# Four edits in a one-core graph network: spare rows for pad slots, a later turn in the mixer, clears inside the rests of GpSimd, and another opening order of the second attend pass

## The reference, cut to what matters

```python
xn = layernorm(x)
x  = x + gnn0(xn, src, dst, edge_weight) + mix0(xn)   # mix0: 4 layers of linear attention and feed-forward
x  = x + moe(layernorm(x))                            # 8 experts, top 2
xn = layernorm(x)
x  = x + gat1(xn, edges (src -> dst)) + mix1(xn)      # gat1: softmax over the edges of each row; mix1: one layer
x  = x + ffn1(layernorm(x))                           # half of the tokens only
```

## Time and profile before

| | us |
|---|---|
| median of 3 runs | 5937.94 (5934.52 to 5938.88) |
| the profiled execution: own time | 5937.63 |
| its span, first to last instruction | 5935.8 |
| busy: TensorE | 5210.6 (88%) |
| busy: GpSimd | 3923.0 (66%) |
| busy: DVE | 3351.1 (56%) |
| busy: ScalarE | 2918.8 (49%) |

### The profile page before, as it was taken

One profiled execution on the slowest core, in us unless ns is written; L12 is line 12 of the kernel. 1 busy time (PEld: TensorE's weight loads), 2 busy tenths in 40 slices (PEclk: granted clock), 3 DMA queues, 4 the chain that ended last, 5 costly groups with the idle time before them and its releaser, 6 DMA issues. The chain is left out here.

```text
span 5935.8 us, 89987 instructions
## 1 busy us (share of the span) xinstructions
PE 5210.6 (88%) x25856; PEld 4404.4 (74%) x25856; DVE 3351.1 (56%) x8788; ACT 2918.8 (49%) x7114; POOL 3923.0 (66%) x6674
## 2 busy tenths in 40 slices
PE   5579999999989999899867999996877887777899
PEld 2468887888878888788756888884556666666788
DVE  8667775444545555443325555555767777776641
ACT  6345554555545555555434333332545555555444
POOL 1677787777666666777747777777457777777000
PEclk8799999999999999999978999997889999999999
DMA  2322112113333333344355122213323343336300
GB/s 68 91 77 52 50 45 64 42 50 111 104 113 95 103 97 103 105 113 113 103 66 158 49 59 54 59 49 97 79 77 104 103 107 103 104 103 96 98 24 33
DMA packets 378209, 493.21 MB, mean 83 GB/s; under 512 B 97664, under 2 KB 315640, under 8 KB 375288
## 3 DMA queue, kind: packets, MB, share of 16 engines
q0 software_dynamic: 135008, 236.92, 16.8%
q1 hardware_dynamic: 242712, 250.54, 14.4%
HBM read 385.16 MB, written 102.04 MB: 82 GB/s over the span
## 5 line engine op out<-in xcount | busy, mean ns | idle before, releaser
L305 POOL DMA_INDIRECT edges_g<-xn_rows,edges_idx x880 | 863.0, 981 | 390.5 <-issue 230.8
L2060 POOL DMA_INDIRECT messages_g<-h_rows,edges_record x880 | 842.9, 958 | 360.1 <-issue 231.0
L248 POOL DMA_INDIRECT sorted_dst<-edges_record,edges_place x784 | 800.8, 1021 | 365.8 <-issue 217.1
L248 POOL DMA_INDIRECT sorted_src<-edges_record,edges_place x784 | 770.6, 983 | 293.9 <-issue 213.7
L1224 PE MATMUL mixer_f_ps<-mixer_f_out,mixer_w 128*128 128x250 f32 x3200 | 755.6, 379 | 16.9 <-issue 15.7
L1235 PE MATMUL mixer_y_ps<-mixer_w,mixer_g 128*125 128x256 f32 x3200 | 724.6, 379 | 0.0
L277 POOL MEMSET edges_idle<- 128x96 f32 x3328 | 621.0, 187 | 144.3
L1224 PEld LDWEIGHTS mixer_f_ps<-mixer_f_out,mixer_w 128*128 128x128 f32 x3200 | 604.6, 193 | 87.1 <-issue 19.0
L1235 PEld LDWEIGHTS mixer_y_ps<-mixer_w,mixer_g 128*125 128x125 f32 x3200 | 593.8, 188 | 85.5
L2232 PE MATMUL messages_s_ps<-messages_g,messages_one 128*128 128x257 f32 x1760 | 456.3, 403 | 112.0 <-DVE messages_one L2143 105.6
L1381 ACT ACTIVATE mixer_g<-mixer_f_ps,mixer_b 128x250 f32<-128x250 f32 x800 | 330.3, 465 | 394.5 <-PE mixer_f_ps L1224 392.6
(11 more groups left out here) (543 smaller groups left out, 10403.2 us busy)
## 6 DMA issues: line engine op xcount, KB each, us to landing
mixer_q<-qT SPq DMA_DIRECT2D x100, 250.0 KB
mix_rows<-mixer_rows SPq DMA_DIRECT2D x100, 250.0 KB
qT<-mixer_qT SPq DMA_DIRECT2D x75, 250.0 KB, 2.9
mixer_rows<-mix_rows SPq DMA_DIRECT2D x75, 250.0 KB
edges_g<-xn_rows,edges_idx POOLq DMA_INDIRECT x880, 3.1
messages_g<-h_rows,edges_record POOLq DMA_INDIRECT x880
sorted_dst<-edges_record,edges_place POOLq DMA_INDIRECT x784
sorted_src<-edges_record,edges_place POOLq DMA_INDIRECT x784
```

The source lines that it names most:

```text
L248: self.nc.gpsimd.indirect_dma_start(self.orders[s][0], bass.IndirectOffsetOnAxis(self.place[s][:, j:j + 1], 0), self.record[s][:, j, :], N ...
L305: self.nc.gpsimd.indirect_dma_start(self.g[n % GR][:, j, 0:D], None, self.table_d, bass.IndirectOffsetOnAxis(self.idx[:, t:t + 1], 0)).the ...
L2060: self.nc.gpsimd.indirect_dma_start(self.g[n % GR][:, j, :], None, self.table_d, bass.IndirectOffsetOnAxis(self.idx[:, t:t + 1], 0)).then_inc(
```

## The change

It makes four edits. (1) Pad slots point at 128 rows of zeros behind row N, one for each lane, in both tables. (2) In the mixer, TensorE does `raise_part(1)` ahead of `rows_turned`, and ScalarE `curve(1)` ahead of `attend_affine`. (3) The two memsets of the sums are gone; the memsets of the rests clear the sums piece by piece (96 columns each) and go on with `idle` once they are through. (4) In `attend_low` SP loads what the fold needs first, the fold comes first on TensorE and DVE, the lists' PSUM tiles are others, and the last steps of the lists (now `look_listed`) stand on DVE at the end of chunk 0.

```diff
-    def pool_pause(self, pool):
-        for _ in range(PAUSES):
+    def pool_pause(self, pool, row=None):
+        sums, width = self.acc[:, :, :].rearrange("p h d -> p (h d)"), HB * (D + 1)
+        for k in range(PAUSES):
             if self.pauses:
                 pool.wait_ge(self.idled, self.pauses)
-            self.nc.gpsimd.memset(self.idle[:, :], 0.0).then_inc(self.idled, 1)
+            at = width if row is None else (row * PAUSES + k) * IDLE
+            tile = self.idle[:, :] if at >= width else sums[:, at:min(at + IDLE, width)]
+            self.nc.gpsimd.memset(tile, 0.0).then_inc(self.idled, 1)
...
         pool.dma_start(rec[:, :, :], self.orders[1][0].rearrange("(p t) c -> p t c", p=P)).then_inc(self.listed, 16)
-        nc.gpsimd.memset(self.acc[:, :, :], 0.0).then_inc(self.listing, 1)
...
+            sp.dma_start(spare[:, :], c_d["iota"][0:1, :].rearrange("o p -> p o")).then_inc(spare_in, 16)
             for to, src in ((kin[1], keys[1]), (win, weights)):
...
-            sp.wait_ge(blanked, 2)
+            sp.wait_ge(blanked, 4)
             for s in S:
                 sp.dma_start(orders[s][0].rearrange("(p t) c -> p t c", p=P), blank[:, :, :]).then_inc(edges.prefilled, 16)
+            sp.dma_start(table_d[N:N + P, :], zeros[:, 0:D]).then_inc(edges.prefilled, 16)
+            sp.dma_start(table2_d[N:N + P, :], zeros[:, :]).then_inc(edges.prefilled, 16)
...
-                    nc.vector.memset(blank[:, :, 1:3], 0.0).then_inc(blanked, 1)
+                    nc.vector.memset(blank[:, :, 2:3], 0.0).then_inc(blanked, 1)
                     nc.vector.memset(blank[:, :, 0:1], -1.0).then_inc(blanked, 1)
+                    nc.vector.memset(zeros[:, :], 0.0).then_inc(blanked, 1)
+                    dve.wait_ge(spare_in, 16)
+                    nc.vector.tensor_scalar(blank[:, :, 1], spare[:, 0:1].to_broadcast([P, ST]), float(N), None, ALU.add).then_inc(blanked, 1)
...
-            nc.gpsimd.memset(edges.acc[:, :, :], 0.0).then_inc(cleared, 1)
-            pool.wait_ge(cleared, 1)
...
+                    if forward:
+                        raise_part(p, m, 1)
                     if attend:
                         rows_turned(n)
-                    if forward:
-                        raise_part(p, m, 1)
                     side(0)
...
                         curve(p, m, 0)
+                    if forward:
+                        curve(p, m, 1)
                     if attend:
                         attend_affine(p, n)
-                    if forward:
-                        curve(p, m, 1)
```

In `attend_low` (SP, then DVE; `first_loads` are ident, wx, 16 pieces of the query and key weights, bx, gain and offset; `loads` are wo, blocks, bo and 8 pieces of wv):

```diff
-            for b in range(3):
+            sp.dma_start(x[0][:, :, :], rows_of(x_d, 0)).then_inc(x_loaded[0], 16)
+            sp.wait_ge(by_head, 2)
+            for to, src in first_loads:
+                sp.dma_start(to[:], src).then_inc(fold_in, 16)
+            for b in range(1, 3):
                 sp.dma_start(x[b][:, :, :], rows_of(x_d, b)).then_inc(x_loaded[b], 16)
...
             for b in range(2):
                 dve.wait_ge(x_loaded[b], 16)
                 ln.dve_stats(dve, b, b)
...
-            dve.wait_ge(listed, 6 * 16)
+            dve.wait_ge(fold_in, 16 * len(first_loads))
+            dve.wait_ge(started, 5)
+            for k in range(2):
+                nc.vector.tensor_scalar(wide_b[:, k, :], ones[:, :], bx[:, k:k + 1], None, ALU.mult).then_inc(prepared, 1)
+            for b in range(2):
+                ln.dve_norm(dve, b, b)
+            dve.wait_ge(listed, 5 * 16)
...
                 if c + 2 < NCH:
                     ln.dve_norm(dve, c + 2, b)
+                if c == 0:
+                    look_listed()
```

More of the change, by code:

```diff
@@ L352, in pairs_of, with open_stage @@
     return pairs[k * share:(k + 1) * share]
-def open_stage(nc, name, x_d, table_d, keys, weights, orders, edges, c_d):
+def open_stage(nc, name, x_d, table_d, table2_d, keys, weights, orders, edges, c_d):
     S = range(2)
@@ L373, in open_stage @@
             "ident_in", "key_in", "turned", "statted", "aggred", "rooted", "inverted", "normed"))
-        blank = ph.sb("blank", [P, ST, 3])
+        blank, spare, zeros, spare_in = ph.sb("blank", [P, ST, 3]), ph.sb("spare", [P, 1]), ph.sb("zeros", [P, D + 2]), ph.sem("spare_in")
         tally_at, before, spot, ahead = ph.sb("tally_at", [P, 2 * FAR + HB], BF16), ph.sb("before", [P, P], BF16), ph.sb("spot", [ROWS2, HB], BF16), ph.sb("ahead", [HB, ROWS2])
@@ L421, in _ @@
                 sp.dma_start(orders[s][1].rearrange("(p j) -> p j", j=PB), bucket_i[s][0:NB, :]).then_inc(saved, 16)
[L422 removed]
+            sp.wait_ge(edges.prefilled, 64)
             sp.wait_ge(saved, 32)
@@ L1711, in queries_turned @@
                 mm.then_inc(qT_made, 1)
-            pe.wait_ge(listed, 6 * 16)
-            pe.wait_ge(lists, 1)
-            nc.tensor.transpose(low_ps[0:1, 0:NT], low[:, :], ident[0:NT, 0:NT]).then_inc(found0, 1)
-            pe.wait_ge(lists, 6)
-            nc.tensor.matmul(low_ps[:, 64:65], spare[0:1, :], least[0:1, 0:1], start=True, stop=True).then_inc(found0, 1)
-            nc.tensor.matmul(a1_ps[:, 0:NPR], a1_rows[:, :], is_bucket[:, :], start=True, stop=True).then_inc(found0, 1)
-            pe.wait_ge(weights, 16 * len(loads))
+            pe.wait_ge(fold_in, 16 * len(first_loads))
             for i in range(2):
@@ L1730, in _ @@
             mm.then_inc(prep, 1)
-            pe.wait_ge(viewed, 1)
             ln.pe_turn(pe, 0, 0)
+            pe.wait_ge(listed, 5 * 16)
+            pe.wait_ge(lists, 1)
+            nc.tensor.transpose(low_ps[0:1, 0:NT], low[:, :], ident[0:NT, 0:NT]).then_inc(found0, 1)
+            pe.wait_ge(lists, 6)
+            nc.tensor.matmul(low_ps[:, 64:65], spare[0:1, :], least[0:1, 0:1], start=True, stop=True).then_inc(found0, 1)
+            nc.tensor.matmul(a1_ps[:, 0:NPR], a1_rows[:, :], is_bucket[:, :], start=True, stop=True).then_inc(found0, 1)
             pe.wait_ge(folded, 2)
@@ L1772, in _ @@
             pe.wait_ge(fed_plus, 1)
+            pe.wait_ge(weights, 16 * len(loads))
             for k in range(2):
@@ L1800, in _ @@
             act.wait_ge(ln.eps_ready, 1)
-            act.wait_ge(weights, 16 * len(loads))
+            ln.act_root(act, 0, 0)
+            act.wait_ge(fold_in, 16 * len(first_loads))
             act.wait_ge(prep, 1)
@@ L1912, in _ @@
-            step(nc.vector.tensor_tensor(rest[:, :], a1_t, look[:, :, 0], ALU.subtract))
-            dve.wait_ge(lists, 11)
-            step(nc.vector.tensor_copy(look[:, :, 1], rest[:, :]))
-            dve.wait_ge(lists, 12)
-            step(nc.vector.tensor_tensor(look[:, :, 2], rest[:, :], look[:, :, 1], ALU.subtract))
-            dve.wait_ge(lists, 13)
-            dve.wait_ge(weights, 16 * len(loads))
-            dve.wait_ge(started, 5)
-            for k in range(2):
-                nc.vector.tensor_scalar(wide_b[:, k, :], ones[:, :], bx[:, k:k + 1], None, ALU.mult).then_inc(prepared, 1)
@@ L1922, in _, with look_listed @@
-            for k in range(2):
-                nc.vector.tensor_scalar(diag[:, k, :], ident[:, :], bo[:, k:k + 1], None, ALU.mult).then_inc(started, 1)
-            for b in range(2):
-                ln.dve_norm(dve, b, b)
+            def look_listed():
+                dve.wait_ge(found0, 3)
+                dve.wait_ge(lists, 8)
+                dve.wait_ge(edge0, 6)
+                nc.vector.tensor_copy(a1_t, a1_ps[:, 0:NPR]).then_inc(viewed, 1)
+                dve.wait_ge(viewed, 1)
+                step(nc.vector.tensor_scalar(ms.a1_c[:, :], a1_t, shift[:, 1:2], None, ALU.add))
+                step(nc.vector.tensor_copy(look[:, :, 0], a1_t))
+                dve.wait_ge(lists, 10)
+                step(nc.vector.tensor_tensor(rest[:, :], a1_t, look[:, :, 0], ALU.subtract))
+                dve.wait_ge(lists, 11)
+                step(nc.vector.tensor_copy(look[:, :, 1], rest[:, :]))
+                dve.wait_ge(lists, 12)
+                step(nc.vector.tensor_tensor(look[:, :, 2], rest[:, :], look[:, :, 1], ALU.subtract))
+                dve.wait_ge(lists, 13)
+                dve.wait_ge(weights, 16 * len(loads))
+                for k in range(2):
+                    nc.vector.tensor_scalar(diag[:, k, :], ident[:, :], bo[:, k:k + 1], None, ALU.mult).then_inc(started, 1)
```

52 lines of the change are left out of this document (23 added, 29 removed).

## The result

The changed kernel takes 5847.61 us (median of 4 runs, 5843.5 to 5850.48), the kernel before 5936.23 in the same runs: ratio 0.9851, 95% interval 0.9837 to 0.9864, so 88.6 us less. The forecast was 5846. In later runs, beside experiments, the two kernels took 5847.41 and 5942.16 (ratio 0.984, 0.9827 to 0.9854).

What follows compares the result with a forecast made beforehand. TensorE was taken to bound the mixer and slow DMA landings its end. The terms -43 - 10.5 - 27 - 6.5 - 8 + 3 = -92, from a median of 5937.94, gave 5846 us; range 5825 to 5878.

Steps and rivals of the forecast that it cites:

- Part 1: Mixer's end: pads on 128 rows land in 2.8 us, not 14.0, removing TensorE's stall; -43, ends -30 and -46.
- The forecast's 1.3: Mixer's end: the margin in us by which GpSimd's own rate just doesn't bind once the gathers land fast.
- Rival (a): Mixer's and forward's ends: pads are slow at any address, so 38.5 us of gain goes, giving 5899; chance 0.08.
- Part 2: Forward stage's end: faster pad gathers and no GpSimd waits on TensorE bring the last batch earlier; -10.5 (-6 to -12).
- Part 3: Mixer's passes: raise_part ahead of rows_turned cuts TensorE's 37.7 us of waits for normed rows; -27, ends -29 and -12.
- the forecast's sign: Mixer: if right, the waits of L793 on the norm are under 10 us in all.
- the 1.7 set aside for `queries_kept`: Mixer: 1.5 to 2 us expected lost because ScalarE makes `queries_kept` later; taken off the 37.7 us of waits.
- rival (b): Another limiter: `queries_kept` late (+15), GpSimd's rate at mixer's end (+13), or fold's opening (+3); 5859 to 5877; chance 0.22.
- the forecast's own 72 turns: Mixer: count of turns with an attention part where TensorE might wait for ScalarE's attend_affine, in the slower-than-before rival, chance 0.03.
- Part 4: Removed memsets: DVE's open-stage chain shortens, -6.5; at the experts' end the next stage begins earlier, -8 (-6 to -10).
- Part 5: Second attend pass's opening: chunk 0 begins 1.6 earlier, but the lists' last steps stand uncovered on DVE; +3 (-3 to +6).

Runs made afterwards that it cites:

- e11: The changed kernel itself with all four edits, run again beside later experiments: 5847.41 us, against 5942.16 for the kernel before (ratio 0.984).
- e6: All four edits, but every pad slot points at the first spare row alone: 6546.58 us, on a chip slower for the kernel before.
- e8: All four edits, but the pad slot of lane p points at live row p, not a spare row: 6501.55 us, same slow chip.
- e9: All four edits, but the pads share 16 spare rows, eight lanes to a row: one run of 5855.05 us.
- e12: All four edits, but x(1) is loaded right behind x(0) and the lists' last DVE steps are spread: 5844.7 us.
- e10: All four edits, but ScalarE keeps its old order, attend_affine then curve(1): 5874.52 us, against 5847.41 for all four edits.
- e1: The kernel before with edit (1) alone, pads at spare rows in both tables: ratio 0.995 against 6586.49 us.
- e2: The kernel before with edit (2) alone, the order in the mixer on TensorE and ScalarE: ratio 0.9959 against 6586.49 us.
- e3: The kernel before with edit (3) alone, clears within the rests: ratio 0.9964 against 6586.49 us.
- e5: Edits (1), (2) and (3), with the second attend pass as before: 6497.14 us, ratio 0.9894 against the kernel before.
- e4: The kernel before with edit (4) alone, the opening of attend_low: ratio 0.9985 against 6586.49 us, inconclusive.

## Why the prediction was right, and where its terms were off

The mechanisms and their places were those forecast; the sum came to -87.2 in the profiled execution against -92, and no rival took over. That the median lies only 1.6 us from the forecast is in part luck: by the rows of the table above, six parts of the forecast came out 11.1 less favourable in all and two 6.3 more.

*Part 1* (mixer's end, -43): -39.8, in e11 -42. The landings are 2.9 as taken, and GpSimd's rate does not bind, by a margin of 2.3. The forecast's 1.3 counted the 0.95 of the issue twice, since the profile's landing runs from the start of the issue; with 2.8 alone the batch is ready at 3032.2 and the margin is 2.3. That this is the measured one is chance: counted from the last gather, the batch and TensorE both came 1.4 later than that. What is short is in two of the sum's small terms. The forecast took away idle times of 2.87 and 1.74, "since side products have their data in time"; the trace puts them to "issue", not to the data, and such idle times remain: in pass 4 they sum to 22.7 before and 20.2 after, one of 5.46 ahead of a side product at 2909.07 among them. And TensorE's busy time in pass 4 fell by 3.6 (560.2 to 556.6) where 5.5 was put down to the lower clock. Rival (a) falls: e6 has the same bytes at one row, and its packets take 0.71 us on the mean where e8's take 0.21. The Trainium skill's fit ("DMA: Bandwidth & Descriptors", "Anatomy of one DMA"), 2.0 us and bytes over 436 GB/s, gives an estimate of 2.3 us for such a gather. That is near the 2.9 of different rows, and far from the 14.0 of one shared row, which the kernel before alone has on record.

*Part 2* (forward's end, -10.5): -11.1. Both its terms hold: from the last gather's start to DVE's last batch it is 6.8 less (9.5 to 2.8), and the two waits of GpSimd on TensorE of 4.8 in all are gone. No landing of these gathers is recorded, so that one is read from DVE. Here too 0.95 was counted twice; without it the term is -11.5.

*Part 3* (-27): -32.7, in three more profiles with the edit (e9, e11, e12) -24 to -35, with a mean over the four of -29. The idle time, which is all that the forecast priced, fell by 25 to 26 in each of them, so the term was sound and 1 to 2 too large. In its pieces: the waits for the normed rows fell by 24.9 (to 12.8, where the forecast's sign was "under 10"), not by 28.7, and the 1.7 set aside for `queries_kept` was hardly needed (2.8 before, 3.0 after). The rest of the -32.7 is busy time of TensorE, which moved the other way in e9 and e11. The bound of 0.4 per turn of rival (b) was near what each wait costs when ScalarE's half is missing (0.33 in e10), but not its count: the forecast's own 72 turns in three passes make 48 in passes 1 and 2, not 37, and e10 has 40 waits there.

*Part 4* (-6.5 and -8): DVE's chain in the open stage is 6.7 shorter (its last COPY_PREDICATED starts at 117.0, not 123.7), as taken, but 4.4 of it reach the first attend pass and 2.9 the mixer. The forecast let the whole stage end earlier with DVE ("DVE bounds the stage from there") and had no term for what follows behind DVE; what takes the rest there was not looked into. In e11, e12, e10 and e9 4.4, 6.1, 3.4 and 10.9 reach the mixer, so the mean over five profiles is 5.5 and the size of this term is that of the spread. The experts' end gave 6.9. Three pieces of it were off: the list's load took 9.5 from its issue to the end of the wait, where some 7 had been estimated with a rate that no row shows; the barrier took 3.0, not 1.4; and GpSimd issued that load 3.0 earlier after the last L2882 than before, for which there was no term. In e11, e10, e9 and e12 the stretch is 23.7, 25.9, 27.1 and 27.4, where after has 23.4 and before 30.3, so -7 was at the lucky end.

*Part 5* (+3): +5.1. The pieces: chunk 0 earlier by 3.7 (1.6 forecast), the list's steps +5.8 in chunk 0 as worked out (12.1 from one key maximum to the next in place of 6.2), and then, where 0.5 to 1 was to come back, a further loss at the lower clock: chunks 4 to 10 take 51.6 in place of 47.4, and the chunks behind them give some 1.5 back. The lower clock may come from TensorE's waiting in the opening, but the kernel before waits there as well (21.1 and 5.3) and gets the higher level sooner, and e12, with other waits, has the clock of after; the cause stays open. The loss of chunk 0 is DVE's, as forecast. In chunks 4 to 10 DVE is no busier than before (40.53 and 40.23) and TensorE is 5.4 us busier, so the pass does not follow DVE alone, as the forecast had it.

What stays open besides: why edit (4) shortened the pass on the chips where the kernel takes 6560 or more (257.2 to 260.5 without it in e1, e2, e3 and e5, 248.5 to 253.6 with it in e4, e6 and e8), and the price of edits (3) and (4) alone at the level of a few us. On those chips edits (1), (2) and (3) also gave less in their own stretches than on the first, and why is not known.

## What to carry to other kernels

Give padding indices of an indirect DMA different rows, even live ones: 16 different rows in 128 lanes were enough here, and the slow gathers cost most by what queues up behind them. When two engines share a hand-written order, move the step on both: with the half on TensorE alone the kernel was 27 us slower than with both. And read a term of the clock in more than one execution before it is given a price: TensorE's busy time in the mixer's first three passes moved by -9.5 to +1.8 us in four profiles, while its idle time fell by 25 to 26 in each.

## What the runs showed of the hardware that was not expected

Gathers whose 128 descriptors read one row, one after another, landed in 14.0 us in place of 2.9, at a DMA share of 0.86 for 97 GB/s where different rows have 0.37 for 109, and with packets of 0.69 us in place of 0.21; at eight descriptors to a row they landed in 2.9. And the kernel before took 10 to 11% longer on two chips (6560 and 6586) than in its other runs (5936 and 5942), with nothing in it changed. In the first attend pass on one of them (e8) the granted clock was 0.83 where it is 0.95 in before and after, and ScalarE's longest idle times (sum, times, longest) have no releaser in the trace:

```profile
ACT attend_qT L981 <- remote: 50.0, 21, 3.2
ACT attend_ek L965 <- issue: 44.5, 17, 4.2
```

What holds ScalarE there was not looked into further.
